# A Flamingo-style block on one core: experts' results combined inside the second attention, in one program without a barrier

## What is computed

```python
x = x + jnp.tanh(g_xattn[0]) * _L0_xattn_ref(_layernorm(x), ctx, ctx, ...)   # 16 heads of 16, softmax over the queries
x = x + jnp.tanh(g_ffn[0])   * _L0_ffn_ref(_layernorm(x), ...)               # 8 experts of 1024, the best 2
x = x + jnp.tanh(g_xattn[1]) * _L1_xattn_ref(_layernorm(x), ctx, ...)        # own keys and context keys, gated per head
x = x + jnp.tanh(g_ffn[1])   * _L1_ffn_ref(_layernorm(x), ...)               # 1 shared + best 3 of 15 experts of 512
```

```python
topk_expert_outputs = jnp.take_along_axis(expert_outputs, gather_idx, axis=2)
mixed_output = jnp.sum(topk_expert_outputs * topk_weights[..., None], axis=2)
```

## Time and profile before

| | us |
|---|---|
| median of 3 runs | 1350.7 (1348.15 to 1351.69) |
| the profiled execution, its own time | 1346.78 |
| span of its instructions | 1345.0 |
| PE busy | 1175.5 (87%) |
| DVE busy | 600.0 (45%) |
| ACT busy | 487.1 (36%) |
| POOL busy | 412.3 (31%) |
| mean granted clock of PE | 0.939 of full |

### The profile page before, as it was taken

One profiled execution on the slowest core, in us unless ns is written; L12 is line 12 of the kernel. 1 busy time (PEld: TensorE's weight loads), 2 busy tenths in 40 slices (PEclk: granted clock), 3 DMA queues, 4 the chain that ended last, 5 costly groups with the idle time before them and its releaser, 6 DMA issues.

```text
span 1345.0 us, 29078 instructions
## 1 busy us (share of the span) xinstructions
PE 1175.5 (87%) x11408; PEld 914.5 (68%) x11408; DVE 600.0 (45%) x1351; ACT 487.1 (36%) x1143; POOL 412.3 (31%) x428
## 2 busy tenths in 40 slices
PE   5999999736999999338999999999989979999970
PEld 3667777536999999324666666665656669999960
DVE  4777767662110101346567656665543501222216
ACT  2445455412333333113444445444433203333321
POOL 3666666602222221230001100100110124555533
PEclk9999999957999999769999999999969999999995
DMA  5111110016999987350000101000000228999965
GB/s 164 28 37 30 31 30 20 8 52 261 338 328 327 331 326 292 113 171 12 13 23 20 30 14 30 19 19 2 8 13 0 79 87 309 354 355 351 348 238 173
DMA packets 64351, 180.92 MB, mean 135 GB/s; under 512 B 10136, under 2 KB 36568, under 8 KB 55768
## 3 DMA queue, kind: packets, MB, share of 16 engines
q1 hardware_dynamic: 56008, 155.07, 33.5%
q0 software_dynamic: 8064, 22.03, 4.5%
q10 hardware_dynamic: 144, 1.97, 0.4%
HBM read 163.11 MB, written 15.93 MB: 133 GB/s over the span
## 4 chain that ended last, share of the span: by engine, by line
PE 44%; DVE 3%; issue 3%; DMA 3%; SPq 1%; ACT 1%; DVEq 0%
PE kept_psum L1839 5%; PE kept_psum L1185 5%; PE kept_psum L1848 5%; PE kept_psum L1129 5%; PE kept_psum L1864 4%; PE kept_psum L1149 4%; PE kept_psum L1101 4%; PE kept_psum L1561 3%; PE kept_psum L1171 3%; PE kept_psum L1116 2%; DVE at_negmax L852 2%; PE kept_psum L1180 1%; DMA ex_xhat<-ex_results 1%; PE kept_psum L1155 1%; DMA ex_shT<-ex_results 1%
## 5 line engine op out<-in xcount | busy, mean ns | idle before, releaser
L1789 ACT ACTIVATE ex_hT<-kept_psum,ex_w 128x128 f32<-128x128 f32 x464 | 132.3, 368 | 321.8 <-PE kept_psum L1839 200.9
L1839 PE MATMUL kept_psum<-ex_xT,ex_w 128*128 128x128 f32 x1856 | 225.2, 278 | 0.1
L1839 PEld LDWEIGHTS kept_psum<-ex_xT,ex_w 128*128 128x128 f32 x1856 | 218.3, 195 | 0.4 <-DMA ex_w<-in_pack_in 0.3
L1848 PE MATMUL kept_psum<-ex_w,ex_hT 128*128 128x256 f32 x928 | 213.9, 379 | 0.0
L1848 PEld LDWEIGHTS kept_psum<-ex_w,ex_hT 128*128 128x128 f32 x928 | 170.1, 190 | 19.8
L1616 POOL DMA_INDIRECT ex_results<-ex_yt,ex_to_row x84 | 82.8, 986 | 258.0 <-DVE ex_yt L1758 258.0
L1019 ACT ACTIVATE at_probs<-kept_psum 120x800 f32<-120x800 f32 (+2 forms) x128 | 101.2, 842 | 71.7 <-PE kept_psum L1155 71.7
L852 DVE TENSOR_REDUCE at_negmax<-kept_psum 100x2 f32<-100x722 f32 x128 | 115.2, 900 | 0.0
L497 ACT ACTIVATE at_probs<-kept_psum 120x800 f32<-120x800 f32 (+1 forms) x96 | 80.1, 836 | 73.3 <-PE kept_psum L609 73.0
L1758 DVE TENSOR_TENSOR ex_yt<-kept_psum,ex_b 128x256 f32<-128x256 f32 x32 | 13.6, 424 | 204.6 <-PE kept_psum L1848 204.6
L1421 POOL TENSOR_TENSOR ex_r<-ex_var,kept_mhalf 100x2 f32<-100x2 f32 x16 | 11.3, 705 | 304.0 <-DVE ex_var L1416 304.0
(11 more groups left out here) (236 smaller groups left out, 1806.6 us busy)
## 6 DMA issues: line engine op xcount, KB each, us to landing
ex_w<-in_pack_in SPq DMA_DIRECT2D x32, 1028.0 KB
ex_w<-in_pack_out SPq DMA_DIRECT2D x32, 1024.0 KB
ex_w<-in_pack_in SPq DMA_DIRECT2D x52, 514.0 KB
ex_w<-in_pack_out SPq DMA_DIRECT2D x52, 512.0 KB
at_ctx<-in_ctxT SPq DMA_DIRECT2D x32, 361.0 KB, 3.2
ex_normed<-ex_xhat SPq DMA_DIRECT2D x16, 200.0 KB
ex_xhat<-ex_results SPq DMA_DIRECT2D x8, 400.0 KB
ex_shT<-ex_results SPq DMA_DIRECT2D x8, 400.0 KB
```

The costliest lines, as they stand in the source:

```text
L1789: last = act.activation(hT[t % N][:, c, :], ps_h[:, (t * U + u) % N, i * P:(i + 1) * P], ACT.Gelu, bias=w1[t % N][:, B1 + c:B1 + c + 1])
L1839: last = pe.matmul(ps_h[:, (t * U + u) % N, i * P:(i + 1) * P], w1[t % N][:, c * ff + f:c * ff + f + P], xT[t % N][:, c, :], start=(c == 0 ...
L1848: last = pe.matmul(ps_y[:, t % N, 0:D], hT[t % N][:, c, :], w2[t % N][:, c * D:(c + 1) * D], start=(c == 0), stop=(c == FC - 1))
```

## The change

**One block.** `build` allocates one SBUF arena and places every tile by hand (a `Pool` is now an address that grows; the second attention's weights lie in 40960 bytes at the top, free all the time). All five programs run in one block. Semaphores of a spent stage are reused; a `Handover` clears them without a barrier: each engine but POOL says `leave`, POOL waits for the four, clears and says so, and each engine waits (`enter`) where it first needs them. There are two: one after the first attention, one for the first experts' semaphores.

```diff
+class Handover:
+    def leave(self, eng):
+        eng.sem_inc(self.left, 1)
+    def clear(self, pool):
+        pool.wait_ge(self.left, 4)
+        ...
+            pool.sem_clear(range(first, last + 1))
+        pool.drain().then_inc(self.cleared, 1)
+    def enter(self, eng):
+        eng.wait_ge(self.cleared, 1)
```

```diff
@@ attend0, sync
+            if t == B - NC:
+                early.load(sp)
@@ experts, tensor
             rank()
+            if early is not None:
+                early.tensor(pe)
...
             table()
+            if early is not None:
+                early.tensor_done(pe)
@@ experts, vector
             for t in range(-1, NT + 1):
+                if early is not None and t == 3:
+                    early.vector(dve)
@@ experts, scalar
                 act.activation(norm_rec[:, :], norm_sum[:, :], ACT.Exp).then_inc(exp_out, 1)
+                early.scalar(act)
@@ attend1, tensor
-        pe.wait_ge(wa_loaded, 32)
+        fed.drained(pe)
+        first.enter(pe)
+        second.leave(pe)
+        for b in range(PRE):
+            values01(b)
+            values2(b)
         for t in STEPS:
+            if t == 2:
+                second.enter(pe)
...
-            if on(t + 2):
+            if on(t + 2) and t + 2 >= NK:
                 project_key(t + 2, 0)
...
+            if on(t) and t >= PRE:
                 values01(t)
```

**Results combined by group.** The ways of the first experts are no longer all added before the second attention. `Fed` hands the four groups (4 batches, 2 choices each) to its programs:

```diff
@@ attend1, vector
-        moments(0)
-        set_masks()
+        first.enter(dve)
+        for b in range(PRE):
+            take_values01(b)
+            take_value2(b)
+        fed.vector(dve, 0)
+        moments(0)
         newton(0)
         normed(0)
         normed(1)
+        fed.vector(dve, 1)
         for t in STEPS:
             if t == -1:
-                scale_rest()
                 dve.wait_ge(filled, 10)
+            if t == 2:
+                second.enter(dve)
...
+            if t in (-1, 0):
+                fed.vector(dve, t + 3)
+            if t == 0:
+                fed.finished(dve)
+                second.leave(dve)
@@ attend1, gpsimd
-        root(0)
+        first.enter(pool)
...
+        fed.gpsimd(pool, 0)
+        root(0)
+        for g in range(1, NG):
+            fed.gpsimd(pool, g)
         for b in range(B + 4):
+            if b == 1:
+                second.clear(pool)
+                prep.fill(pool)
@@ attend1, scalar
+        fed.scalar(act, 0)
+        fed.scalar(act, 1)
...
+            if t < 0:
+                fed.scalar(act, t + 4)
@@ attend1, sync
+        fed.ways(sp)
...
+            if t == 1:
+                fed.finished(sp)
+                second.leave(sp)
+                second.enter(sp)
+                prep.load(sp)
```

More of the change, by code:

```diff
@@ L14 @@
+import math
 from contextlib import ExitStack
@@ L691, in attend1 @@
+def attend1(nc, m, consts, psum, xs, prep, early, fed, first, second):
     ident, mhalf, tanhg = consts.ident, consts.mhalf, consts.tanhs[:, 1:2]
@@ L739, in attend1 @@
     STEPS = range(-2, B + 4)
-    ring = [(n, t + off) for t in STEPS for n, off in ORDER if on(t + off)]
+    ahead = [(n, b) for b in range(PRE) for n in ("value01", "value2")]
+    ring = ahead + [(n, t + off) for t in STEPS for n, off in ORDER if on(t + off) and (n, t + off) not in ahead
+                    and not (n in ("key0", "key1") and t + off < NK)]
     ring_at = {use: i for i, use in enumerate(ring)}
@@ L1290, in __call__ @@
         self.eng.wait_ge(self.sem, self.n)
+@dataclass
+class Fed:
+    ways: Callable
+    gpsimd: Callable
+    vector: Callable
+    scalar: Callable
+    summed: Callable
+    finished: Callable
+    drained: Callable
 @dataclass
@@ L1538, in main @@
         weighted, last_added = m.sem("weighted"), m.sem("last_added")
-        weighted_row = [m.sb(f"weighted{i}", [T, D]) for i in range(2)]
         def shared_bank(n):
@@ new lines, in weight_last, with summed @@
+        def weight_last(act, g):
+            for i in range(g * top, (g + 1) * top):
+                b = g * GB + GB - 1
+                act.wait_ge(ways_in[i % PARTS_N], 16 * (i // PARTS_N + 1))
+                need(act, last_added, i - 1)
+                act.activation(weighted_row[i % 2][:, :], parts[i % PARTS_N][:, GB - 1, :], ACT.Copy,
+                               scale=gates[:, i % top, b:b + 1]).then_inc(weighted, 1)
+        def summed(eng, g):
+            eng.wait_ge(added, (g + 1) * top * (GB - 1))
+            eng.wait_ge(last_added, (g + 1) * top)
@@ L1925, in build @@
[L1925 to L1935 removed]
+        top = Pool(nc, "at1", nc.sbuf_usable_end // 32 * 32 - EARLY_BYTES)
@@ new lines, in build @@
+        e0 = Pool(nc, "ex0", p0.at)
+        second0, fed = main0(e0, early)
+        after0 = Handover(kept, "first", m0.allocated)
+        after1 = Handover(kept, "second", p0.allocated + e0.allocated)
+        p1 = Pool(nc, "ex1", kept.at, p0.allocated + e0.allocated)
+        prep1, main1 = experts(nc, p1, consts, psum, xs, "ex1", out, a["L1_ffn_gW"], a["L1_ffn_gb"], a["pack1_in"], a["pack1_out"], a["L1_ffn_rb2"],
+                               3, 512, [a[f"L1_ffn_{n}"] for n in ("sW1", "sb1", "sW2", "sb2")])
@@ new lines, in build @@
+        m1 = Pool(nc, "at1", p1.at, m0.allocated)
+        first1 = attend1(nc, m1, consts, psum, xs, prep1, early, fed, after0, after1)
+        e1 = Pool(nc, "ex1", p1.at, p1.spent + m1.spent)
+        second1, _ = main1(e1)
+        leave = Programs(after0.leave, after0.clear, after0.leave, after0.leave, after0.leave)
+        run(nc, first0, leave, second0, first1, second1)
+        nc.clear_and_free_semaphores([sem for m in (kept, top, p0, m0, e0, p1, m1, e1) for sem in m.owned])
+        nc.all_engine_barrier()
```

413 lines of the change are left out of this document (226 added, 187 removed).

## The result

The changed kernel takes **1338.05 us** (median of 11 runs, 1330.95 to 1339.79), the kernel before, run beside it, 1348.63 (11 runs, 1342.18 to 1352.66): ratio 0.9926 [0.9906, 0.9947]. Faster, as forecast, but by 10.6 us instead of 21.5, and 0.05 us beyond the upper end of the range. The profiled execution took 1332.8 us, its span is 1331.1 (before: 1346.8 and 1345.0).

A forecast was written before the change was run, and what follows sets the result against it. PE was taken as nearly full except in troughs, notably 37.7 us idle behind the first experts. Terms -20.5 - 3 + 3.5 - 1.5 = -21.5 us, from 1350.7 to 1329.2 us; range 1322 to 1338.

The forecast's parts named there:

- Up to the first maxima: Second attention's start: batch 0 normalised at 566.8 instead of 589.6, first maxima 26.4 us earlier at half clock.
- Step -1: Batch 0's maxima: 2.9 us for half clock, 3.5 for group 2's additions; `take_max(0)` at 591.7, 20.5 us earlier.
- Steps 0 and 1: Second attention: 3 us gained, up to 3.5 given back in step 0, 1.5 gained in step 1; total -21.5 us.
- +3 of gain: Step 0: with batch 2's keys and batch 0's values gone, DVE's earlier maxima release the second unit of scores.
- 3.5 for group 3: End of step 0: group 3's additions on DVE give back up to 3.5 us.
- half clock until step 2: Rival for second attention: sparse step 0 units take 6 us instead of 4.6; gain near 13, 1337.7 us; chance 0.15.
- At nothing: Early keys fit PE's 12.93 us idle ahead of the table; masks, scaling, loads and second handover hidden, no cost.
- the rival of the binding handover: POOL's clearing ends after PE's step 2 begins; with 25 us of clearing, -11: 1339.7 us; handover or early piece: 0.05.

The follow-up runs named there:

- useless matmuls in the steps alone: Changed kernel plus result-less identity matmuls on PE in steps -2 to 0, none of the 40 ahead of the first turning: 1328.67 us, ratio 0.9853.
- other places: Changed kernel with group 2's additions moved to the end of step -2, group 3's behind batch 1's first maxima: 1332.03 us, ratio 0.9888.
- the fastest kernel: Changed kernel with other places for the additions plus identity matmuls, 40 ahead of the first turning and more in steps -2 to 0: 1321.29 us, ratio 0.9827.
- the kernel with all three: Changed kernel with keys of batches 1 and 2 back in steps -1 and 0, other places, and identity matmuls ahead and in steps: 1326.67 us, ratio 0.9853.
- the kernel with the 40 ahead: Changed kernel plus only 40 identity matmuls ahead of the first turning, none in steps -1 and 0: 1332.51 us, ratio 0.9909.

## Why the prediction was wrong

**Up to the first maxima: right.** The normalised x, the values behind the experts (5.73 us), the clock at half from about 560: all within 0.6 us. The barrier, the wait for weights and six of eight additions were off the path, as said.

**Step -1: right but for 1.4 us.** Half clock and group 2's additions (the maxima took 14.1 us, not 12.8; the additions 3.05, not 3.5) made `take_max(0)` 42.5 us behind the experts instead of 41.1.

**"Steps 0 and 1": the step that failed.** I carried the half clock through step -1 and then dropped it. For step 0 I took +3 of gain for the missing keys and values against 3.5 for group 3, so 22.3 us. It took 30.2. The clock is 6.5 of the 7.9 between them: with the clock restored (useless matmuls in the steps alone) the step takes 23.7. Group 3's additions are 2.0, not 3.5 (other places: 28.2). The rest is the gain of 3 from the missing keys and values, which wasn't there (7.9 = 6.5 - 1.5 + 2.9). The premise under it, that the missing keys are a gain at PE, has the wrong sign as long as the clock is low: putting them back gained 4.3 us. What their absence is worth at full clock no run shows, since there useless matmuls stand in their place. Step 1 was to gain 1.5 and lost 1.4, with the clock down again at 640, and step 2 lost 1.0, where I had set nothing.

The evidence was in the rows. In the earlier trace rows the stretch from 977.5 to 990 was at 0.50 with PE busy for 76% of it; I used it for the start-up and for the rival, but not for my step 0. The sparse stretch at 1.00, with PE at two thirds, came right behind dense keys, and these were what the change moved away. The Trainium skill, TensorE: Matmul & The Clock Gate, section "What's actually happening", says that activity releases the throttle. The trace agrees only in part: the clock rose between 616 and 620 (0.84 there, 1.00 behind), after PE had been busy without idle time since 612.75, but not in the 7.3 us without idle time from 577.25. The sketches in its section "Loop structure matters more than you think" count VectorE's copy out of PSUM as harmless for the clock where the next matmuls follow immediately, and give a long wait for DMA as the bad case. Here the next matmuls do not follow immediately: the waits inside 588 to 616 are for DVE and ACT, 0.5 to 2.3 us each, with the DMA share at 0.00, and the clock stayed at half. So it isn't waits for DMA alone that count.

**The rival "half clock until step 2"** is nearly what happened (the clock was at half through step 0 and once more at the end of step 1), and its time (1337.7) is that of the median to 0.4 us. That is partly luck. Its step 0 is right: 21.8 + 5.6 + 3.5 = 30.9 us, measured 30.2. But it had 1.4 too much of gain in `take_max(0)`, 2.9 in step 1 and 1.0 in step 2: 13 us of gain where the stretch has 8.2. The medians differ by 10.6, 2.4 of them outside the stretch, and the kernel before came out 2.1 us lower than the 1350.7 from which the rival's time was counted. Its chance should have been above that of the forecast.

**At nothing:** right. The early keys took 9.0 us of 12.93; the masks and scaling ran from 334.40 to 338.44, and PE turned tile 5 at 341.00, no later than before. The second handover bound nothing: POOL had cleared and was filling at 625.72, 17 us before PE's step 2 (642.3). Two slips bear on nothing: the routing trough of the earlier trace rows is in slices 9 and 10, not 8 and 9, and the rival of the binding handover adds up to -11.5, not -11.

```profile
338.36 0.41 DVE L1901 COPY ex_xT<-kept_psum 128x256 f32<-128x256 f32 x1
```

```profile
625.72 0.20 POOL L1508 MEMSET ex_ones<- 100x128 f32 x1 [37.12 <-issue]
```

**Left open:** what makes the time outside this stretch differ between executions by several us. The granted clock at the ends of stages has a part in it: over the first 12 us of the second attention's last step it was 1.00 in the fastest kernel, where the step took 21.8 us, and 0.72 in the kernel with all three, where it took 24.5. This wasn't tried by itself.

## What to carry to other kernels

Before you take matmuls out of a sparse stretch, ask what holds the clock there: for each stretch that becomes sparse, price every matmul at both levels, and take the higher level only where a row shows it at that sparseness without dense work ahead. Where PE, DVE and ACT wait for each other in a ring, half clock can last (56 us here); useless matmuls inside the ring's gaps repaid their cost here (-6.6 and -8.8 us at batch 4), those ahead of it alone did nothing in the trace, and those in a nearly full step made it 2.2 us longer. Small additions on DVE belong into the idle time ahead of its first wait, not in front of the operation that everyone waits for (3.8 us directly, 6.3 with what followed).

## What the runs showed that I had not expected

- Half clock lasted for 56 us with PE busy 60 to 73% of the time, and 1.00 was kept at 81% (19.47 of 24 us).
- Half clock outlasted 7.3 us of PE without idle time (scores, a projection and scores, 577.25 to 584.59).
- The clock full until 568 was half a few us later, in the kernel with the 40 ahead, with PE busy 15 of 20 us.
- More matmuls made the stretch shorter three times over: keys put back, useless ones in the steps, and both kinds with other places.
- From step 3 on the steps of the second attention repeat to 0.1 us across kernels (22.9, 23.0, 23.1, 23.6, 23.1, 23.7, ...), except the last (21.8 to 24.6). The others that differ are step 0 (21.6 to 30.2), step 1 (21.3 to 25.5) and step 2 (22.9 to 23.8).
